# Contexts by head in halves of the array's columns, and content that reads q in its stored order

## What is computed

```
qkv = einsum('bcxy,oc->boxy', img, w_qkv);  q, k, v = split(qkv)
k = softmax(k, axis=-1)                              # over the 4096 pixels
context = einsum('ndm,nem->nde', k, v)               # 64 x 64 for each head
content_out = einsum('nde,ndm->nem', context, q)
Sx = einsum('ndxy,xid->nixy', q, Px);  Yh = einsum('nixy,neiy->nexy', Sx, v)
Yh = batch_norm(Yh)                                  # statistics over all images and heads
Sy = einsum('ndxy,yid->nixy', q, Py)
rel_pos_out = einsum('nixy,nexi->nexy', Sy, Yh)
out = einsum('bcxy,oc->boxy', content_out + rel_pos_out, w_out) + b_out
x = x + out
```

## Time and profile before

| | us |
|---|---|
| median of 3 runs | 2912.08 |
| lowest and highest | 2909.36, 2917.21 |
| the profiled execution | 2908.83 |
| its span, first to last instruction | 2907.0 |
| PE busy | 2596.9 (89%) |
| DVE busy | 2017.8 (69%) |
| ACT busy | 1689.4 (58%) |
| POOL busy | 1402.7 (48%) |
| stage 1, stage 2 in the span | 1806, 1101 |

### The profile page before, as it was taken

The page is one execution under the profiler, slowest core; times in us unless marked ns, Lnnn a source line. Parts: engine busy times, 40 slices in busy tenths (PEclk is TensorE's granted clock), DMA queues, the critical chain, the costliest instruction groups (busy, mean ns, idle before and its releaser), DMA issues. The chain is left out here.

```text
span 2907.0 us, 119666 instructions
## 1 busy us (share of the span) xinstructions
PE 2596.9 (89%) x54900; PEld 2105.4 (72%) x54900; DVE 2017.8 (69%) x3126; ACT 1689.4 (58%) x2984; POOL 1402.7 (48%) x617
## 2 busy tenths in 40 slices
PE   4899999899899999999999996689899898989897
PEld 3787787787687787787777785667676767666674
DVE  7577677677667667667667655787677768677774
ACT  3655655655555565565565564566565656566563
POOL 0424424424434344334344343776766767676761
PEclk9999999999999999999999998799999999999999
DMA  2423523522532542532544335577768777777763
GB/s 99 128 72 82 156 62 88 144 68 75 141 83 68 132 99 69 141 90 68 127 104 119 94 87 121 133 196 194 186 179 229 177 207 172 214 194 197 187 172 109
DMA packets 448615, 382.35 MB, mean 132 GB/s; under 512 B 307312, under 2 KB 374128, under 8 KB 448112
## 3 DMA queue, kind: packets, MB, share of 16 engines
q1 hardware_dynamic: 429680, 341.14, 46.7%
q10 hardware_dynamic: 18432, 33.56, 3.2%
HBM read 205.79 MB, written 168.82 MB: 129 GB/s over the span
## 5 line engine op out<-in xcount | busy, mean ns | idle before, releaser
L843 POOL TENSOR_TENSOR k_f<-k_f,negmax 128x1024 f32<-128x1024 f32 x128 | 303.3, 2397 | 858.7 <-DVE negmax L810 858.7
L456 PE MATMUL bank<-w_hi,x_hi 128*128 128x256 f16 x2048 | 572.0, 279 | 11.0 <-DVE x_lo L735 7.7
L456 PE MATMUL bank<-w_hi,x_lo 128*128 128x256 f16 x2048 | 565.4, 276 | 3.8 <-issue 3.8
L456 PE MATMUL bank<-w_lo,x_hi 128*128 128x256 f16 x2048 | 566.2, 276 | 0.0
L1290 POOL TENSOR_TENSOR x_f<-x_f,ones 128x1024 f32<-128x1024 f32 x127 | 287.2, 2261 | 227.7 <-DMA x_f<-y_scratch 223.2
L1242 DVE TENSOR_TENSOR yb_lo<-x_f,yb_hi 64x1024 f16<-64x1024 f32 x192 | 367.5, 1914 | 31.8 <-ACT yb_hi L1156 28.8
L750 DVE TENSOR_TENSOR v_lo<-bank,v_hi 128x256 f16<-128x256 f32 x512 | 214.0, 421 | 249.5 <-ACT v_hi L598 246.7
L597 ACT ACTIVATE k_f<-bank 128x256 f32<-128x256 f32 x512 | 200.5, 392 | 289.1 <-PE bank L456 287.6
L456 PEld LDWEIGHTS bank<-w_hi,x_hi 128*128 128x128 f16 x2048 | 297.0, 145 | 22.5 <-issue 15.0
L456 PEld LDWEIGHTS bank<-w_lo,x_hi 128*128 128x128 f16 x2048 | 299.7, 146 | 2.3
L456 PEld LDWEIGHTS bank<-w_hi,x_lo 128*128 128x128 f16 x2048 | 297.5, 145 | 2.6
(11 more groups left out here) (152 smaller groups left out, 8312.7 us busy)
## 6 DMA issues: line engine op xcount, KB each, us to landing
y_scratch<-yst SPq DMA_DIRECT2D x256, 256.0 KB, 4.7
x_f<-y_scratch SPq DMA_DIRECT2D x256, 256.0 KB, 6.3
q<-q_scratch SPq DMA_DIRECT2D x256, 256.0 KB, 4.9
x_f<-x SPq DMA_DIRECT2D x64, 512.0 KB, 5.8
q_scratch<-q_hi SPq DMA_DIRECT2D x128, 256.0 KB
q_scratch<-q_lo SPq DMA_DIRECT2D x128, 256.0 KB
x_res<-x SPq DMA_DIRECT2D x128, 256.0 KB, 6.1
out<-x_res ACTq DMA_DIRECT2D x128, 256.0 KB, 4.2
```

What stands on the lines that cost most here:

```text
L456: mm = pe.matmul(outs, lhs[a], rhs[m], start=first and n == 0, stop=last and n == 2, **kw)
L843: pool.tensor_tensor(kk, kk, negmax[:, :].unsqueeze(1).to_broadcast([P, 8, P]), ALU.add).then_inc(shifted, 1)
```

## The change

Three edits belong together in stage 1. `v_hi` and `v_lo` now hold each head's 64 channels with its own two columns of ones, 66 in a row. `context_piece` issues two matmuls where there was one: for each head 64 stationary columns, 66 moving columns, and 64 partitions of the result. Nothing is computed any more that mixes the heads. `context_out` finds both heads' contexts in the same columns and needs two instructions over 128 partitions in place of four over 64, so the counts of the semaphore `ctx_out` fall from 6 to 4 per pair, and SP's wait for them with it. The readers and writers of v (L534, L598, L750) address the new layout, in as many instructions as before.

The fourth edit is in stage 2. `content` reads q in its stored order a, y, x, without a step, and addresses the columns of the result in that order. Of two neighbouring moving columns one now goes to row x and the other to row x + 1 of the bank, 64 fp32 columns apart.

```diff
-            VW = P + 2
-            v_hi = sb("v_hi", [P, 2, HALF, VW], F16, p1)
+            VW = DK + 2
+            v_hi = sb("v_hi", [P, 2, HALF, 2, VW], F16, p1)
...
                     for y2 in range(4 * piece, 4 * piece + 4):
                         for k, (a, m) in enumerate(TERMS):
-                            mm = pe.matmul(ctx_ps[:, 0:VW], (p_hi, p_lo)[a][:, y2, :],
-                                           (v_hi, v_lo)[m][:, hp % 2, y2, :],
-                                           start=(y2 == 0 and k == 0), stop=(y2 == HALF - 1 and k == 2))
+                            for h in range(2):
+                                own = slice(h * 64, h * 64 + 64)
+                                mm = pe.matmul(ctx_ps[own, 0:VW], (p_hi, p_lo)[a][:, y2, own],
+                                               (v_hi, v_lo)[m][:, hp % 2, y2, h, :],
+                                               start=(y2 == 0 and k == 0), stop=(y2 == HALF - 1 and k == 2))
...
-                for g in range(2):
-                    s = slice(g * 64, g * 64 + 64)
-                    dve.tensor_scalar(cst_parts[s, 0, :], ctx_ps[s, g * 64:g * 64 + 64], cden[s, 0:1], None,
-                                      ALU.mult).then_inc(ctx_out, 1)
...
+                dve.tensor_scalar(cst_parts[:, 0, :], ctx_ps[:, 0:DK], cden[:, 0:1], None, ALU.mult).then_inc(ctx_out, 1)
+                dve.wait_ge(ctx_out, t * 4 + 4)
+                dve.scalar_tensor_tensor(cst_parts[:, 1, :], ctx_ps[:, 0:DK], cden[:, 0:1], cst_parts[:, 0, :],
+                                         ALU.mult, ALU.subtract).then_inc(ctx_out, 1)
...
-                                    both = bank[:, banks[j], :].rearrange("p (a x g y) -> p g a x y", x=XB, g=2, y=HALF)
+
+                                    both = bank[:, banks[j], :].rearrange("p (a x g y) -> p g a y x", x=XB, g=2, y=HALF)
                                     for g in range(2):
                                         for h in range(2):
                                             mm = pe.matmul(both[h * 64:h * 64 + 64, g], context[:, hp % 2, h, :],
-                                                           q2[:, hp % 2, h, g, 4 * (i + j):4 * (i + j) + 4, :, :]
-                                                           .rearrange("p a y x -> p a x y"),
+                                                           q2[:, hp % 2, h, g, 4 * (i + j):4 * (i + j) + 4, :, :],
```

More of the change, by code:

```diff
@@ L388, in store_context @@
                 def store_context(t):
-                    sp.wait_ge(ctx_out, t * 6 + 7)
+                    sp.wait_ge(ctx_out, t * 4 + 5)
                     sp.dma_start(c_dram[t].rearrange("k p e -> p k e"), cst_parts[:, :, :]).then_inc(ctx_st, 16)
@@ L534, in turn @@
                                             mm = pe.matmul(bank[own, banks[g], j * 64:j * 64 + 64],
-                                                           (v_hi, v_lo)[a][half, hp % 2, y2, own],
+                                                           (v_hi, v_lo)[a][half, hp % 2, y2, h2, 0:DK],
                                                            (sx_hi, sx_lo)[m][half, h2 * HALF + y2, :],
@@ L597, in turn @@
                             act.activation(k_f[:, hp % 2, 2 * i:2 * i + 2, :], v[:, :, 0, :], ACT.Copy)
-                            act.activation(v_hi[:, hp % 2, 2 * i:2 * i + 2, 0:P], v[:, :, 1, :],
+                            act.activation(v_hi[:, hp % 2, 2 * i:2 * i + 2, :, 0:DK],
+                                           v[:, :, 1, :].rearrange("p j (h e) -> p j h e", h=2),
                                            ACT.Copy).then_inc(hi_done, 1)
@@ L634, in context_out @@
                 dve.wait_ge(ctx_st, t * 16 + 16)
-                dve.reciprocal(cden[:, :], ctx_ps[:, P:P + 1]).then_inc(ctx_out, 1)
-                dve.wait_ge(ctx_out, t * 6 + 2)
+                dve.reciprocal(cden[:, :], ctx_ps[:, DK:DK + 1]).then_inc(ctx_out, 1)
+                dve.wait_ge(ctx_out, t * 4 + 2)
                 dve.tensor_scalar(cden[:, :], cden[:, :], factors[:, 0:1], None, ALU.mult).then_inc(ctx_out, 1)
-                dve.wait_ge(ctx_out, t * 6 + 3)
-                for g in range(2):
-                    s = slice(g * 64, g * 64 + 64)
-                    dve.tensor_scalar(cst_parts[s, 0, :], ctx_ps[s, g * 64:g * 64 + 64], cden[s, 0:1], None,
-                                      ALU.mult).then_inc(ctx_out, 1)
[L643 to L647, removed]
+                dve.wait_ge(ctx_out, t * 4 + 3)
+                dve.tensor_scalar(cst_parts[:, 0, :], ctx_ps[:, 0:DK], cden[:, 0:1], None, ALU.mult).then_inc(ctx_out, 1)
+                dve.wait_ge(ctx_out, t * 4 + 4)
+                dve.scalar_tensor_tensor(cst_parts[:, 1, :], ctx_ps[:, 0:DK], cden[:, 0:1], cst_parts[:, 0, :],
+                                         ALU.mult, ALU.subtract).then_inc(ctx_out, 1)
             @block.vector
             def _(dve):
[L651 to L654, removed]
+                dve.memset(v_hi[:, 0, :, :, DK:VW], 1.0).then_inc(init, 1)
+                dve.memset(v_hi[:, 1, :, :, DK:VW], 1.0).then_inc(init, 1)
+                dve.memset(v_lo[:, 0, :, :, DK:VW], 0.0).then_inc(init, 1)
+                dve.memset(v_lo[:, 1, :, :, DK:VW], 0.0).then_inc(init, 1)
                 dve.sem_inc(freed, BANKS)
@@ L749, in turn @@
                             v = src.rearrange("p (j t n) -> p j t n", j=2, t=2)
-                            dve.tensor_tensor(v_lo[:, hp % 2, 2 * i:2 * i + 2, 0:P], v[:, :, 1, :],
-                                              v_hi[:, hp % 2, 2 * i:2 * i + 2, 0:P], ALU.subtract).then_inc(freed, 1)
+                            dve.tensor_tensor(v_lo[:, hp % 2, 2 * i:2 * i + 2, :, 0:DK],
+                                              v[:, :, 1, :].rearrange("p j (h e) -> p j h e", h=2),
+                                              v_hi[:, hp % 2, 2 * i:2 * i + 2, :, 0:DK], ALU.subtract).then_inc(freed, 1)
                             if i % 8 == 7:
```

4 lines of the change are left out of this document (2 added, 2 removed).

## The result

| | before | after |
|---|---|---|
| median of 5 runs, us | 2912.64 | 2939.18 |
| lowest and highest | 2909.36, 2917.21 | 2931.64, 2945.15 |
| the profiled execution | 2908.83 | 2933.93 |
| stage 1, stage 2 in the span | 1806, 1101 | 1801, 1131 |

The account below looks back on a forecast made before the run. PE, busy 89% of the span, was taken as the bound, with stops. Stage 1's -32 and stage 2's +67 us gave +35 on 2908.83, so 2944, and 2947 us for the median; range 2866 to 2985 us (8 in 10).

Parts of the forecast that it names:

- The bound and the nature of the stops: Whole kernel: PE bounds it, busy 89% of the span; its stops inside stage 1 items are late instruction packets.
- Contexts on PE, -89 us: Stage 1: context halves run side by side at 0.030 us against 0.057, saving 83 us, and layout changes save 6.
- Instructions added, 1.8 us per pair late, 58 us: Stage 1: 192 more instructions per pair, 0.75 packet, outrun the fetch and come 1.8 us late per pair.
- Net -32 us: Stage 1: 2.8 us saved on PE less 1.8 us late instructions, -1.0 us for each of 32 pairs.
- the rest of stage 1 at nothing: Stage 1: fewer DVE instructions in context_out and the new shape of v for ACT and DVE cost nothing.
- Content pair at 0.216 us, +108 us on PE: Stage 2: the stepped write doubles a content pair from 0.108 us, +0.105 us for each of 1024 pairs.
- The analogy with sy's read: Stage 2: sy's jumping read takes 0.06 us a pair against sx's 0.03, so the stepped write should cost a factor of two.
- 10/16 of it on the path, +67 us: Stage 2: six of an image's 16 content groups hide under the wait for sy_lo; the others lengthen PE's path.
- The sum: Whole kernel: -32 us in stage 1 and +67 us in stage 2 give +35 us; median forecast 2947 us.
- Free and half-price writes: Stage 2 rivals: the stepped write costs nothing, 2878 us, chance 0.26; or 0.16 us a pair, 2914 us, chance 0.13.
- serial halves: Stage 1 rival: context halves don't run side by side, 2 x 0.03 us as before, about 3010 us; chance 0.03.
- The rival of late instructions: Stage 1 rival: all added instructions are late, so stage 1 gains nothing, +3 us, 2982 us in all; chance 0.08.

Follow-up runs that it names:

- e10: Kernel before with one line of order changed: where sx and kv alternate by two items, the two kv items stand ahead of the two sx; 2875.1 us, ratio 0.9851.
- e3: Contexts in column halves, each head over every second pixel block only, so no matmuls added and half of each sum omitted, against the kernel before; 2828.0 us, ratio 0.9699.
- e2: The context edits alone, content as in the kernel before, against that kernel; 2907.3 us, ratio 0.9967 (0.9952 to 0.9983).
- e8: Kernel before, but content reads and writes two neighbours at a time, the next two 256 fp32 away, results in wrong places; 2909.7 us, ratio 0.9985.
- e1: The content edit alone (q in stored order, stepped write), contexts as in the kernel before, against that kernel; 2952.7 us, ratio 1.0126.
- e4: Contexts in halves, content as before, one context piece moved behind each of kv items 8 to 15, against the kernel before; 2960.5 us, ratio 1.0148.
- e6: Whole contexts and content as in the kernel before, one context piece moved behind each of kv items 8 to 15, against that kernel; 2964.7 us, ratio 1.0176.

## Why the prediction was right, and where it was not

- **The bound and the nature of the stops: right.** e10 shows it: nothing but the order of dense and sparse items differs from the kernel before, and 43 us go. e3 agrees, and so do the packets, of which one ends 1.2 to 1.6 us before PE goes on at each of the stops inside q, yh, contexts and items of sx.
- **Contexts on PE, -89 us: nearly.** The pace by the rows is 0.032 us and not 0.030, and contexts and layout changes together gave 84 us. The halves run side by side and q to context is 0.21 us, both as forecast.
- **Instructions added, 1.8 us per pair late, 58 us: right in size.** Stops grew by 62 us, with 24 packets more: 46 us inside contexts, 10 in q, 4 in yh, all places that it named.
- **Net -32 us: wrong, it was -5 between the two traces and -10 (-5 to -14) by e2's runs.** 9 us of the difference are the two sizes above. The step that failed is "the rest of stage 1 at nothing": I costed a stop at its own length. Behind stops in the crowded run the granted clock fell, and q took 10 us longer, in the kernel after and in e2. What is left of the difference between the two traces is mostly kv's 7 us, which the runs with the old stage 1 show without any edit.
- **Content pair at 0.216 us, +108 us on PE: right.** Measured 0.21 and +97 us. The analogy with sy's read was sound by luck more than by reason: e8 shows that two neighbours are enough for the write, while sy's read has two and is at half pace.
- **10/16 of it on the path, +67 us: the hiding worked in the way said, but for less, and the result was +30.** The wait for `sy_lo` gave back 29 us by the distances (forecast 41), so 97 - 29 = 68 stood on the path, near 67 only because the content was 11 us cheaper and the hiding 12 us smaller. Then 25 us came back where the clock behind the stalls was at 2.4 GHz again, or by the time L1124 ran, and 12 us through fewer stops. Here the failed step is the same: a stall costed at its own length. The 0.93 of stage 2's clock stood in the earlier trace rows, and no term used it. It stood behind the stalls that the edit shortened.
- **The sum: right by luck, because two errors cancelled.** Stage 1 came out 22 to 27 us dearer than forecast, stage 2 cheaper by 37. The one omission that is in both is the clock behind a stop, with opposite signs: +10 in stage 1, -25 in stage 2. The rest are the sizes above and, in stage 2, the 12 us of fewer stops.
- **The rivals.** Free and half-price writes fell by the pair's 0.21 us, serial halves by the 0.03 us. The rival of late instructions had stage 1 at +3, and -5 is nearer to that than to my -32; but it wanted 2.9 us of stops more in each pair, and they were 62 / 32 = 1.9.
- **Left open.** Why a packet of instructions takes 3.3 us at the least (the smallest distance between two in either trace is 3.29), and how much the other DMA traffic adds to it, was not tried. That the lower clock follows from the stops is read from rows of several kernels, and no run changed it alone.

## What to carry to other kernels

Count instructions per us as well as PE time: where a run of small matmuls asks for more than PE's instruction queue delivers (65 to 77 per us here), splitting a matmul in two gains little by itself (10 us here, of 84 saved on PE), and an item with few instructions put ahead of the dense one does (43 us here for one line). Before an item is moved, list what it stood in front of: a layout that changes anyway, a broadcast that waits for maxima, a half that another engine still makes. And cost a stop with the clock that follows it, in both directions.

## What the runs showed of the hardware that was not expected

- PE stops inside a product, with no semaphore in the program, when a packet of its instructions is late: all 47 such stops before and all 94 after (stage 1, inside runs of q, yh and contexts and inside items of sx) end 1.2 to 1.6 us after the end of one of these packets, where 7 or 8 in 100 random moments do.
- Single fp32 results 64 fp32 apart halve PE's pace, 0.21 us for 256 columns against 0.11 (e1); runs of two neighbours with a step of 256 fp32 between the runs do not (e8).
- Behind a stop PE's granted clock could be near half for some time (0.66 in the 4.75 us around and behind the stop that ended at 774.46, 0.50 from 2316.6 on), and the stepped write slows with it: content groups behind long stalls took up to 2.9 us against 1.50.
- A change between the array used whole and in halves costs about 0.1 us at each edge, and nearly nothing where another layout change stood already: 0.35 us for the two edges of a piece in kv (e4) against 0.17 for a whole one (e6), and 0.03 between q and yh.
